# Where the second products stand in the slots of a Gelu expert layer

## The chip, the cores and the metric

The kernel runs on one core of one Trainium2 chip. The metric is the device time of one execution in microseconds (us), taken as the median of several runs. The engines are named as in the profile: PE is the matrix engine (PEld its weight loads), ACT the scalar engine, DVE the vector engine, POOL the engine that adds the accumulators here, SP the queue that issues most of the DMAs.

## The reference

The whole is a two-layer block on an input of 32 images x 256 channels x 14 x 14 in float32: a convolution by codebooks with batch norm, a top-2 mixture of 32 experts, a gated squeeze-and-excite stage, and, last, the expert layer that the change touches. Cut to that layer:

```python
h = x @ Wm + bm                                  # 6272 tokens x 256
t = h.reshape(bs * L_ * H, HD)                   # 8 heads of 32 each
w = softmax(t @ expert_emb)                      # 16 experts
topw, topi = top_k(w, 2)
hmid = gelu(einsum('td,edi->tei', t, W1) + b1)   # 128 hidden numbers for each expert
eo = einsum('tei,eio->teo', hmid, W2) + b2
comb = (take_along_axis(eo, topi) * topw).sum(1)
out = comb.reshape(bs, L_, d) @ Wo + bo
```

## The kernel before

All earlier stages run first. The stage of the change ("Gelu stage") computes all 16 experts for every token and head, and weights the outputs with gates that are zero outside the top two.

**Tiling.** The work is cut into 49 units of 1024 columns (256 tokens x 4 heads; the last one 128 tokens x 8 heads). A unit has 4 groups of 4 experts, so there are 196 groups (`NG`) and 784 first products (`m` counts them). Each of these is one expert on 1024 columns:

- `first(m)` (L2258): two matmuls of 512 columns into one of three PSUM tiles `psA[m % 3]`. Because there are three tiles, it waits until the Gelu of product m-3 is done (the wait on `Q["gel"]` in L2263).
- The Gelu (ACT, L2326) of 1024 columns, from `psA[m % 3]` into `hid[m % 8]`. Every fourth one first waits until the second products of the group two back are done, because it overwrites their input.
- `second(g, b)` (L2269): the second products of group g for one of two blocks of 512 columns; four experts side by side in four column strips of the array, into `psY[use % 2]`. It needs the four Gelus of its group, and the DVE must have read what stood in that `psY` tile two uses before.
- `weigh` (DVE, L2347): reads `psY`, adds the bias, multiplies with the gates, writes `gacc` or `gsum`. POOL adds these up (L2254).

**Slots.** PE, DVE and SP walk through 201 slots by hand-written order. In slot k PE issues the four first products of group k (here called f0 to f3) and the two second blocks of group k-1 (s0 and s1). Some slots hold more, each through one use of `psY`: a `fold` (L2280, the sum over the four strips, one per unit, after f2), a `last` (L2291, the output product, two per unit pair, after f0), a `route` (L2314, transposing the gates of a later chunk, 14 in this stage, after f0).

**Order in a slot.** `apart(k)` (L2179) says whether a slot's second blocks stand apart. They do in a slot without extras, and in one whose only extra is a fold and whose successor has no `last`: there the order is f0 f1 f2 s0 f3 s1. In all others it is f0 f1 f2 s0 s1 f3. Of slots 3 to 194, whose lengths the prediction adds up, 84 have no extra (all apart), 48 a fold (24 apart), 46 a `last` (none apart), 14 a `route` (none apart).

The loop that issues them on PE:

```python
for e in range(4):
    if k < NG:
        first(4 * k + e)
    ...
    if e == 2 and "fold" in EXTRAS[k]:
        fold(FOLD[k], EXTRA_USE["fold", k])
    for b in range(NB if 0 < k <= NG else 0):
        if e == (2 + b if apart(k) else 2):
            second(k - 1, b)
```

Of the kernel before, what the change touches and what calls it, by code (L numbers as in the profile page):

```python
# [44 lines left out]
def wait(eng, sem, value):  # L45

    if not (isinstance(value, int) and value <= 0):
        eng.wait_ge(sem, value)
# [33 lines left out]
def build(nc, x, c1T, c2T, c3T, invts, lut1, lut2, lut3, bn1, bn2, bn3, routerT, w_moe,  # L82
          se_w1T, se_b1, se_w2T, se_b2, se_wgT, se_bg, wm, bm, emb, w1, b1, w2, b2, wo, bo, out):
    with ExitStack() as ctx:
# [812 lines left out]
        with phase() as c2:  # L897
# [20 lines left out]
            with nc.Block() as block:  # L918
                @block.gpsimd
                def _(eng):  # L920
                    eng.memset(nm[:], 0.0).then_inc(S["one"], 1)
                    eng.wait_ge(S["one"], 1)
                    eng.memset(nm[:].rearrange("p s (q x) -> p (s q) x", x=32)[:, :, 16:18], 1.0).then_inc(S["one"], 1)
                    for t in range(T):
                        wait(eng, S["y"], t + 1)

                        wait(eng, S["nsc"], (t - 1) * 2)
                        eng.tensor_copy(y_r[:, t % 2], y[:, t % 3]).then_inc(S["yr"], 1)
# [727 lines left out]
        def route_pe(eng, r, use):  # L1656

            wait(eng, Q["rt"], (r + 1) * RT2)
            wait(eng, Q["got"], use if r < EARLY else use - 1)
            for s in range(NSUB):  # L1660
                m = eng.transpose(gates_ps(use)[:, s * SUB:(s + 1) * SUB],  # L1661
                                  route_tile(r, M1)[:, s * NH:(s + 1) * NH].rearrange("p h e -> p (h e)"), ident[0:SUB, 0:SUB])
            m.then_inc(Q["put"], 1)
# [486 lines left out]
        LAST = {8 * c + 11 + m_: (c, m_) for c in range(len(PARTS) - 1) for m_ in range(2)}  # L2150
# [18 lines left out]
        EXTRAS, EXTRA_USE, BLOCK_USE, uses = {}, {}, {}, EARLY  # L2169
# [6 lines left out]
                BLOCK_USE[k - 1, b] = uses  # L2176
                uses += 1

        def apart(k):  # L2179

            return not EXTRAS[k] or (EXTRAS[k] == ["fold"] and k + 1 not in LAST)

        def done_group(g):

            return BLOCK_USE[g, NB - 1] + 1 if g >= 0 else 0
# [32 lines left out]
        with nc.Block() as block:  # L2218
# [37 lines left out]
            @block.tensor  # L2256
            def _(eng):
                def first(m):  # L2258
                    w = m // 16
                    if m % 16 == 0:  # L2260
                        wait(eng, q_stk[w % 2], (w // 2 + 1) * 64)

                    wait(eng, Q["gel"], m - 2)  # L2263
                    for b in range(NB):
                        mm = eng.matmul(psA[m % 3][:, b * BLK:(b + 1) * BLK], w1_r[:, m % 16],  # L2265
                                        x_r[:, w % 2, b * BLK:(b + 1) * BLK], start=True, stop=True)
                    mm.then_inc(Q["mm1"], 1)

                def second(g, b):  # L2269
                    use = BLOCK_USE[g, b]  # L2270
                    wait(eng, Q["gel"], 4 * g + 4)

                    wait(eng, Q["got"], use - 1)
                    for e in range(4):
                        mm = eng.matmul(psY[use % 2][32 * e:32 * e + 32, :], w2_s[:, g % 4 * 4 + e],  # L2275
                                        hid[:, (4 * g + e) % 8, b * BLK:(b + 1) * BLK], start=True, stop=True,
                                        tile_position=(0, 32 * e))
                    mm.then_inc(Q["put"], 1)

                def fold(w, use):  # L2280
                    tok, n, head, heads = UNITS[w]

                    wait(eng, Q["acc"], 3 * w + 3)
                    wait(eng, Q["got"], use - 1)
                    for q in range(heads):
                        mm = eng.matmul(psY[use % 2][q % 4 * 32:q % 4 * 32 + 32, q // 4 * n:(q // 4 + 1) * n], foldm[:],  # L2286
                                        gacc[:, w % 2, q * n:(q + 1) * n], start=True, stop=True,
                                        tile_position=(0, q % 4 * 32))
                    mm.then_inc(Q["put"], 1)

                def last(c, m_, use):  # L2291
                    n = PARTS[c][1]

                    wait(eng, Q["got"], max(use - 1, EXTRA_USE["fold", 4 * min(2 * c + 1, NU - 1) + 6] + 1))
                    for h in range(2):
                        mm = eng.matmul(psY[use % 2][:, 0:n], wo_s[:, h, m_ * 128:(m_ + 1) * 128], comb[:, h, 0:n],  # L2296
                                        start=(h == 0), stop=(h == 1))
                    mm.then_inc(Q["put"], 1)

                for k in range(SLOTS):  # L2300
                    if k == 1:
                        eng.wait_ge(Q["w2"], 16)
                    if k == min(LAST):
                        eng.wait_ge(Q["wo"], 16)
# [3 lines that stand above are left out]
                        if e == 0 and "last" in EXTRAS[k]:  # L2308
                            last(*LAST[k], EXTRA_USE["last", k])
                        if e == 0 and "route" in EXTRAS[k]:  # L2310
                            route_pe(eng, ROUTE[k], EXTRA_USE["route", k])
                        if e == 2 and "fold" in EXTRAS[k]:
                            fold(FOLD[k], EXTRA_USE["fold", k])
                        for b in range(NB if 0 < k <= NG else 0):  # L2314
                            if e == (2 + b if apart(k) else 2):
                                second(k - 1, b)

            @block.scalar
# [109 lines left out]
```

## Time and profile before

| | |
|---|---|
| median of 3 runs | 2380.0 us (2377.41 to 2391.9) |
| span of the profiled execution | 2466.2 us |
| PE busy | 2088.2 us, 85% of the span |
| DVE busy | 1331.5 us, 54% |
| ACT busy | 1290.4 us, 52% |
| POOL busy | 818.1 us, 33% |
| Gelu stage, first to last Gelu | 1560.8 to 2455.9 us |

The profiled execution has no time of its own beside its span; it is 86 us (3.6%) longer than the median of the runs. The Gelu stage is a good third of the span. In it PE and ACT are both nearly always busy, so a share of busy time does not tell which of them sets the pace; the order of single instructions does.

### The profile page before, as it was taken

To read this page: it belongs to the slowest core of one execution; us is meant where nothing else is said; L and a number is where in the kernel's file an instruction comes from. 1 tells how busy PE (TensorE), PEld (TensorE's weight loads), DVE (VectorE), ACT (ScalarE), POOL (GpSimd) and SP (SyncE) were. 2 spreads that over 40 slices of the span, in tenths; PEclk is the share of its full clock that TensorE was granted. 3 is DMA by queue.
4 is the path that set the end of the run, shared out by engine and by line. 5 is a ranking of instruction groups with operands and counts; after the bars stand their busy time and mean duration, and the time that the engine had idled before them with its cause. 6 is when DMAs were issued, how large, how long until landed. Compare 5 with 4: busy or idle time off the path is not lost. (4 is left out here: it accounts for less than half of the span.)

```text
span 2466.2 us, 36023 instructions
## 1 busy us (share of the span) xinstructions
PE 2088.2 (85%) x12850; PEld 1155.0 (47%) x12851; DVE 1331.5 (54%) x2117; ACT 1290.4 (52%) x1634; POOL 818.1 (33%) x608
## 2 busy tenths in 40 slices
PE   6998699997975653788289887799999999999998
PEld 3444355554544442577155554344444444444443
DVE  5666435554555554122166675366666766666633
ACT  2444222222542221122134342698989989988997
POOL 4332211120005554000657511234434334334343
PEclk8999779998996665899578896899999999999999
DMA  2010211212523331576323311555565655556554
GB/s 54 27 34 8 85 59 59 69 55 85 198 89 107 104 100 43 161 209 198 95 64 114 105 59 60 143 162 158 163 162 153 163 155 159 159 160 163 155 151 117
DMA packets 280563, 281.24 MB, mean 114 GB/s; under 512 B 44998, under 2 KB 261654, under 8 KB 280278
## 3 DMA queue, kind: packets, MB, share of 16 engines
q1 hardware_dynamic: 246422, 233.49, 33.8%
q0 software_dynamic: 12288, 25.72, 3.5%
q10 hardware_dynamic: 21696, 19.93, 2.4%
q8 instruction: 99, 1.62, 0.3%
q14 instruction: 58, 0.48, 0.1%
HBM read 203.76 MB, written 75.25 MB: 113 GB/s over the span
## 5 line engine op out<-in xcount | busy, mean ns | idle before, releaser
L2326 ACT ACTIVATE BIG<-psA,b_s 128x1024 f32<-128x1024 f32 x784 | 809.8, 1116 | 89.8 <-PE psA L2265 82.2
L2254 POOL TENSOR_TENSOR BIG<-BIG 128x1024 f32<-128x1024 f32 x147 | 359.6, 2446 | 553.1 <-DVE BIG L2347 553.1
L2265 PE MATMUL psA<-x_r,w_r 128*128 128x512 f32 x1568 | 480.4, 427 | 20.4 <-DMA x_r<-hs_d 12.2
L2347 DVE SCALAR_TENSOR_TENSOR BIG<-psY,b_s,BIG 128x512 f32<-128x512 f32 x392 | 291.6, 749 | 247.6 <-PE psY L2275 246.8
L2265 PEld LDWEIGHTS psA<-x_r,w_r 128*128 128x128 f32 x1568 | 269.0, 190 | 330.5 <-ACT BIG L2326 244.9
L2275 PE MATMUL psY<-BIG,w_s 128*32 128x512 f32 x3136 | 400.9, 602 | 2.9 <-DVE BIG L2347 2.2
L1199 POOL DMA_INDIRECT xg_d<-xnb,SLOT x128 | 131.6, 1028 | 144.2 <-issue 75.4
L719 DVE TENSOR_REDUCE b_nm<-psN 112x32 f32<-112x512 f32 x128 | 83.1, 686 | 148.3 <-PE psN L616 147.8
L1774 POOL DMA_INDIRECT gath<-yg_d,SLOT x128 | 129.9, 1015 | 83.8 <-issue 42.9
L2275 PEld LDWEIGHTS psY<-BIG,w_s 128*32 128x32 f32 x3136 | 73.6, 108 | 160.9 <-issue 91.3
L719 DVE TENSOR_REDUCE a_nm<-psN 98x32 f32<-98x512 f32 x128 | 82.3, 685 | 90.8 <-PE psN L607 90.6
L1535 PE MATMUL ps<-BIG,xv 128*128 x528 | 127.1, 384 | 2.6 <-ACT xv L1561 2.0
L557 POOL CAST b_pat_r<-BIG 72x3584 fp32r<-72x3584 f32 x16 | 50.8, 3172 | 219.7 <-PE psN L616 212.4
L1561 ACT ACTIVATE xv<-ps 128x512 f32<-128x512 f32 x66 | 39.4, 597 | 156.9 <-PE ps L1521 156.9
L580 PE MATMUL ps<-BIG,b_wb 72*128 72x392 f32 x256 | 100.9, 540 | 3.9 <-DVE xv L725 3.9
L1535 PEld LDWEIGHTS ps<-BIG,xv 128*128 128x128 f32 x528 | 96.2, 192 | 14.5 <-issue 3.9
L775 ACT ACTIVATE b_exs<-ps 128x1568 f32<-128x1568 f32 x32 | 47.3, 1477 | 104.5 <-PE ps L585 104.5
L616 PE MATMUL psN<-b_wb_r,b_pat_r 73*112 73x128 f32 x512 | 70.7, 285 | 9.6 <-POOL b_pat_r L557 8.9
L1454 PE MATMUL psN<-ones_c,MS 98*32 98x1 f32 x128 | 6.7, 182 | 82.2 <-DVE MS L1269 72.2
L1576 DVE COPY ex<-ps 128x512 f32<-128x512 f32 x33 | 22.8, 692 | 99.0 <-PE ps L1535 99.0
L616 PEld LDWEIGHTS psN<-b_wb_r,b_pat_r 73*112 73x112 f32 x512 | 61.1, 193 | 30.6 <-DVE b_nm L719 13.4
L1521 PE MATMUL ps<-ident,xv 128*128 128x128 f32 x264 | 41.5, 282 | 39.8 <-DMA xv<-xg_d 25.0
(394 smaller groups left out, 3242.9 us busy)
## 6 DMA issues: line engine op xcount, KB each, us to landing
BIG<-wt_d SPq DMA_DIRECT2D x784, 128.0 KB, 3.2
x_r<-hs_d SPq DMA_DIRECT2D x196, 128.0 KB, 3.5
xg_d<-ex SPq DMA_DIRECT2D x64, 264.0 KB, 3.6
xv<-xg_d SPq DMA_DIRECT2D x66, 256.0 KB, 3.1
BIG<-ypad_d SPq DMA_DIRECT2D x140, 120.0 KB
xv<-x SPq DMA_DIRECT2D x64, 196.0 KB, 2.6
hs_d<-xv SPq DMA_DIRECT2D x32, 392.0 KB
yg_d<-ex ACTq DMA_DIRECT2D x33, 256.0 KB, 3.6
```

The lines of the kernel that those rows point to most:

```text
L557: eng.tensor_copy(pat_r[0:KP].rearrange("p g (b r) -> p g b r", b=IMGS), pat[s % 3][:, :, :, 0:HH * PADW]).then_inc(S["vr"], 1)
L580: eng.matmul(ps4[:, i, 0:CH], w_, src, start=True, stop=False)
L616: mm = eng.matmul(psN[0:SR, bank, g * 128:(g + 1) * 128], pat_r[0:KR, bank * 4 + g, sub * SR:(sub + 1) * SR], wb_r[0:KR, bank * 4 + g], st ...
L719: eng.tensor_reduce(dst, src, AX.X, ALU.max, negate=True).then_inc(S["max"], 1)
L1199: eng.indirect_dma_start(xg_d.ap(), bass.IndirectOffsetOnAxis(ap=SLOT[:, t * NSUB + s, j:j + 1], axis=0), xnb[:, t % XB, s], None).then_in ...
L1535: m = eng.matmul(psZ[:, u, r * C:(r + 1) * C], xt[:, u, r, h * 128:(h + 1) * 128], w_moe_s[:, bass.ds(e * (2 * C) + h * C, C)], start=(h = ...
L1774: eng.indirect_dma_start(gath[:, c % GB, 2 * s + j], None, yg_d.ap(), bass.IndirectOffsetOnAxis(ap=SLOT[:, c * NSUB + s, j:j + 1], axis=0) ...
L2254: eng.tensor_tensor(gacc[:, w % 2], gacc[:, w % 2], gsum[:, a % 2], ALU.add).then_inc(Q["acc"], 1)
L2265: mm = eng.matmul(psA[m % 3][:, b * BLK:(b + 1) * BLK], w1_r[:, m % 16], x_r[:, w % 2, b * BLK:(b + 1) * BLK], start=True, stop=True)
L2275: mm = eng.matmul(psY[use % 2][32 * e:32 * e + 32, :], w2_s[:, g % 4 * 4 + e], hid[:, (4 * g + e) % 8, b * BLK:(b + 1) * BLK], start=True, ...
L2326: eng.activation(hid[:, m % 8], psA[m % 3][:], ACT.Gelu, bias=b1_s[:, m % 16:m % 16 + 1]).then_inc(Q["gel"], 1)
L2347: eng.scalar_tensor_tensor(out=dst, in0=psY[use % 2][:], scalar=b2_s[:, g % 4:g % 4 + 1], in1=wb[:, g % 3, b * BLK:(b + 1) * BLK], op0=ALU ...
```

## The change

The function `apart` goes, and with it the distinction between slots. In every slot both second blocks are issued behind the fourth first product: f0 f1 f2 f3 s0 s1. The extras stay where they were (a `last` or a `route` behind f0, a `fold` behind f2, so now ahead of f3). No instruction is added or removed, and no wait is changed; the uses of `psY`, the order on DVE, POOL, ACT and SP stay as they are.

```diff
-        def apart(k):
-
-            return not EXTRAS[k] or (EXTRAS[k] == ["fold"] and k + 1 not in LAST)
-
...
                         if e == 2 and "fold" in EXTRAS[k]:
                             fold(FOLD[k], EXTRA_USE["fold", k])
                         for b in range(NB if 0 < k <= NG else 0):
-                            if e == (2 + b if apart(k) else 2):
+                            if e == 3:
                                 second(k - 1, b)
```

## Rows read from the trace of the kernel before

**Rows 1.** The page: busy shares, and the chain that ended last by line.

```profile
PE 2088.2 (85%) x12850; PEld 1155.0 (47%) x12851; DVE 1331.5 (54%) x2117; ACT 1290.4 (52%) x1634; POOL 818.1 (33%) x608
PE psA L2265 16%; PE psY L2275 15%; PE psY L2296 2%; ACT BIG L2326 1%; PE psY L2286 1%; DMA rt<-ex_d 0%; PE psY L1661 0%; SPq L2215 0%; SPq L2205 0%; POOLq L2218 0%; POOL BIG L2254 0%; DVE BIG L2347 0%; DVE rs L1625 0%; DVE ex L2356 0%; SPq L2225 0%
```

**Rows 2.** Busy time by stretch: us, then each engine, TensorE's granted clock, DMA.

```profile
54.00:250.00 196.00, 177.61 (x1721) 95.38 (x1720) 125.96 (x159) 85.72 (x117) 59.31 (x50) 0.99 0.08 22
925.00:1014.00 89.00, 32.87 (x166) 26.97 (x166) 28.34 (x85) 10.54 (x21) 31.01 (x32) 0.55 0.22 66
1017.00:1180.00 163.00, 137.69 (x728) 113.38 (x726) 43.07 (x63) 35.84 (x60) 4.83 (x12) 0.98 0.69 202
1577.00:2451.00 874.00, 865.43 (x5239) 382.56 (x5237) 540.88 (x713) 793.11 (x768) 353.27 (x145) 1.00 0.59 157
```

**Rows 3.** Timeline of PE from 2099.81 us on: start, length, instruction and count.

```profile
2099.81 1.67 PE L2265 MATMUL psA<-x_r,w_r 128*128 128x512 f32 x6
2101.41 0.64 PE L2286 MATMUL psY<-BIG,fold 128*32 128x256 f32 x8
2101.87 1.04 PE L2275 MATMUL psY<-BIG,w_s 128*32 128x512 f32 x8
...
2104.50 1.67 PE L2265 MATMUL psA<-x_r,w_r 128*128 128x512 f32 x6
...
2107.76 1.06 PE L2275 MATMUL psY<-BIG,w_s 128*32 128x512 f32 x8
2108.75 1.67 PE L2265 MATMUL psA<-x_r,w_r 128*128 128x512 f32 x6
2110.35 1.07 PE L2275 MATMUL psY<-BIG,w_s 128*32 128x512 f32 x8
2111.35 0.73 PE L2265 MATMUL psA<-x_r,w_r 128*128 128x512 f32 x2
2112.01 1.06 PE L2275 MATMUL psY<-BIG,w_s 128*32 128x512 f32 x8
2113.01 0.74 PE L2265 MATMUL psA<-x_r,w_r 128*128 128x512 f32 x2
...
2114.97 1.92 PE L2275 MATMUL psY<-BIG,w_s 128*32 128x512 f32 x16
2116.83 1.66 PE L2265 MATMUL psA<-x_r,w_r 128*128 128x512 f32 x6
2118.76 0.74 PE L2265 MATMUL psA<-x_r,w_r 128*128 128x512 f32 x2 [0.27 <-ACT BIG L2326]
```

**Rows 4.** Timeline of PE, a slot with a last and the slot behind it.

```profile
2126.49 1.20 PE L2265 MATMUL psA<-x_r,w_r 128*128 128x512 f32 x4
2127.53 1.02 PE L2296 MATMUL psY<-ex,wo_s 128*128 128x256 f32 x4
2128.20 1.28 PE L2265 MATMUL psA<-x_r,w_r 128*128 128x512 f32 x4
2129.41 1.92 PE L2275 MATMUL psY<-BIG,w_s 128*32 128x512 f32 x16
2131.27 1.67 PE L2265 MATMUL psA<-x_r,w_r 128*128 128x512 f32 x6
2133.21 0.74 PE L2265 MATMUL psA<-x_r,w_r 128*128 128x512 f32 x2 [0.28 <-ACT BIG L2326]
2133.88 1.06 PE L2275 MATMUL psY<-BIG,w_s 128*32 128x512 f32 x8
```

**Rows 5.** Timeline of ACT, the Gelus of the same slots; in brackets the idle time before.

```profile
2105.33 11.64 ACT L2326 ACTIVATE BIG<-psA,b_s 128x1024 f32<-128x1024 f32 x11 [0.56 <-PE psA L2265]
2117.59 4.13 ACT L2326 ACTIVATE BIG<-psA,b_s 128x1024 f32<-128x1024 f32 x4 [0.62 <-PE psA L2265]
```

**Rows 6.** Timeline of ACT, the first Gelu of slot 3 and of slot 195.

```profile
1577.39 1.12 ACT L2326 ACTIVATE BIG<-psA,b_s 128x1024 f32<-128x1024 f32 x1 [0.73 <-PE psA L2265]
...
2451.06 3.12 ACT L2326 ACTIVATE BIG<-psA,b_s 128x1024 f32<-128x1024 f32 x3
```

**Rows 7.** Timeline of PE, PEld and DVE, slot 34, which has a fold.

```profile
1717.61 0.64 PE L2286 MATMUL psY<-BIG,fold 128*32 128x256 f32 x8
...
1718.06 2.16 PE L2275 MATMUL psY<-BIG,w_s 128*32 128x512 f32 x16
1718.59 0.41 DVE L2356 COPY ex<-psY 128x256 f32<-128x256 f32 x1
1719.12 0.19 PEld L2275 LDWEIGHTS psY<-BIG,w_s 128*32 128x32 f32 x8 [0.93 <-ACT BIG L2326]
```

**Rows 8.** Timeline of DVE: both weighs of a slot, and a routing step.

```profile
2130.65 1.51 DVE L2347 SCALAR_TENSOR_TENSOR BIG<-psY,b_s,BIG 128x512 f32<-128x512 f32 x2 [1.57 <-PE psY L2275]
...
2132.78 2.38 DVE L1636 TENSOR_TENSOR rt<-rt,rs 98x512 f32<-98x512 f32 x1
```

## The prediction

> **What bounds the kernel now.** I first read the page: PE is the busiest engine, and the chain that ended last runs through PE alone in the Gelu stage, half first products (16% of the span), half second products (15%), with 1% of Gelus [rows 1]. That is not enough, since in this stage ACT works 793 us of 874 and PE's records cover 865 [rows 2]. So I went to the timeline and looked at starts, not at durations, because matmuls overlap.
>
> A plain slot (no extra, order f0 f1 f2 s0 f3 s1) can be read there without a gap: three first products at 2108.75, s0 at 2110.35, f3 at 2111.35, s1 at 2112.01, the next f0 at 2113.01 [rows 3]. That is 1.60 + 1.00 + 0.66 + 1.00 = **4.26 us**, and no idle time stands beside a row: PE sets the pace. ACT could go faster: four Gelus in a row take 4.13 us to the last one's end, one takes 1.12 [rows 5, 6], so their starts lie (4.13 - 1.12)/3 = 1.00 apart and four need 4.01.
>
> A first product costs more alone than in a run, (1.67 - 0.73)/2 = 0.47 for each one added to a run against 0.66 from its start to the next second block [rows 3]; both second blocks in a row take 1.86 (2114.97 to 2116.83) against 2 x 1.00 apart [rows 3]. Changing between the two kinds costs PE time, and the old order changes twice as often as the new one.
>
> The granted clock is 1.00 over the whole stage, the higher of its two levels, 2.4 GHz [rows 2].
>
> **The change part by part.** *PE's work.* The new plain slot is three first products up to a change, 1.60, one more in the run, 0.47, both blocks, 1.86: 3.93 us, a third of a microsecond less than now. If PE or ACT alone set the pace, the slot would fall to about 4.01.
>
> *The new chain.* But f3 may not start before the Gelu of f0 is done (three `psA` tiles), and now both blocks queue behind f3 in PE's order, and the next slot's f0 behind them. So a ring closes once per slot: f3, s0, s1, next f0, its Gelu, next f3. In the old order each ring passes through only one block. Its links, from rows of slots that already have both blocks together:
> - f3 alone to the start of s0: 0.67 (2133.21 to 2133.88, a first product that also came out of a wait on ACT) [rows 4];
> - s0 to the next first product: 1.86 [rows 3];
> - f0 to the start of its Gelu: 0.83 (2104.50 on PE, 2105.33 on ACT, ACT idle before) [rows 3, 5];
> - start of a Gelu to the first product that waits for it: 1.17 (2117.59 to 2118.76, PE idle 0.27 before) [rows 3, 5].
>
> Together **4.53 us**, above both 3.93 and 4.01: the ring sets the pace, and PE waits some 0.6 us a slot ahead of f3. A plain slot gets 0.27 longer. The third link is the uncertain one: for the Gelu after 2116.83 it is 0.76 (to 2117.59), but that one isn't the first of its group and has no second wait [rows 3, 5]; I take 0.83, with 0.76 as the lower bound (4.46).
>
> *Slots with a route* (14). Today f0, route, f1, f2 take 1.96 (2113.01 to 2114.97) [rows 3]; with f3 in the run and both blocks PE needs 1.96 + 0.47 + 1.86 = 4.29, less than the ring, so 4.53.
>
> *Slots with a fold* (48). f0 to fold is 1.60 and the fold takes 0.46 until s0 (2101.41 to 2101.87), its records 0.64 [rows 3]. How long from a fold to a first product isn't shown; between these, say 0.55. Then f3 starts 2.15 behind f0, where the ring alone would let it at 0.83 + 1.17 = 2.00. The slot is 4.53 + 0.15 = 4.68 (4.59 to 4.77). The apart ones take 4.69 now (2099.81 to 2104.50) [rows 3], so nothing changes there. The others gain: with both blocks directly behind the fold, s1 waits for the DVE's copy of the fold where that is late, as in slot 34, where the weights of the second block start at 1719.12 after a copy at 1718.59 [rows 7]; behind f3 that copy is done in time.
>
> *Slots with a last* (46). PE is the bound there: 4.78 from 2126.49 to 2131.27 [rows 4]. In the new order f0 to last is 1.04 - 0.47 = 0.57, last to the end of f1 f2 1.88, f3 0.47, the blocks 1.86, also 4.78; f3 starts about 2.35 behind f0, later than the 2.00 of the ring, so the ring has slack and nothing changes.
>
> *What else is moved.* No DMA, no wait and no DVE, POOL or SP instruction changes its place; the uses of `psY` keep their order. s1 still ends the slot, so the Gelu that waits for s1 to free `hid`, and the gates that SP loads, see it at the same place in the slot. I cost these at nothing; DVE's reading of `psY` is a rival below. What PE saves in changes (0.33 a slot) ends in its wait ahead of f3. In the last slots, before the drain, f3 comes ahead of the blocks, which is worth under 1 us once.
>
> *The sum.* From the first Gelu of slot 3 to that of slot 195 the profile has 2451.06 - 1577.39 = 873.67 us [rows 6], 192 slots. Afterwards: 84 + 14 slots at 4.53 = 443.9, 48 at 4.68 = 224.6, 46 at 4.78 = 219.9, together 888.4. The difference is **+14.7 us** on a span of 2466.2, 0.6%. So the plain slots lose some 0.25 on 84, and a third of it comes back in folds and routes that already had the bad order. Bounds: the third link at 0.76 takes 6.9 off, the fold's ends 4.3 either way, so +3.5 to +19.
>
> The span is 3.6% above the median of 2380.0, and I can't see in it where unprofiled runs save. Spread evenly, 14.7 becomes 14, and the forecast is **2394 us**. If it is the hand-overs between engines that the profile stretches, the ring (4.53 x 0.965 = 4.37) shrinks while PE's 4.26 stays: 98 x 0.16 = 16 off, about -1, or 2379.
>
> **The rivals.**
> *PE's saving counts.* If the ring's hand-overs were so short that it closes in 4.01, ACT would be the bound in 98 slots: 98 x 0.52 = 51 us less than in my sum and thus 36 below now, 2344. To be faster by 1% the ring has to close below some 4.14, that is 0.39 less than the rows give. Against it: the slots with both blocks together already show ACT idle 0.62 ahead of a Gelu and PE idle 0.28 ahead of a first product [rows 4, 5]; for it, only that a profile may stretch hand-overs.
>
> *The clock falls.* PE now waits in every plain slot. If that dropped TensorE to 1.2 GHz in stretches, PE's 3.93 would approach 7.86, 3.3 above the ring; with a tenth of the 98 slots hit, 33 us come on top of 14, 2427 us. It decides from some 3 slots (10 us) onwards, the point at which the time passes +1%. For it: in the stretch from 925 us, where PE is busy 32.87 of 89, the clock is 0.55. Against it: from 1017 us PE is busy 137.69 of 163, 84%, at 0.98, and from 54 us 91% at 0.99 [rows 2]; the new slot would be at 3.93/4.53 = 87%. The Trainium skill ("TensorE: Matmul & The Clock Gate", A second HAM failure mode: psum-queue depth-cycling) speaks against the change here: frequent short idles of PE between groups of matmuls, as the PSUM tiles are cycled, can make the clock oscillate. The stretches named bear it out little.
>
> *`psY` holds up the blocks.* With s0 and s1 together, both weighs come together on DVE, 1.24 behind s0 (2129.41 to 2130.65), 1.51 for both [rows 4, 8]. The next s0 comes 4.53 behind this one and needs the first weigh, done at 1.24 + 0.75 = 1.99: 2.54 to spare. A routing step takes up to 2.38 between weighs [rows 8]; two of the longest in a slot (4.76) against DVE's free 4.53 - 1.51 = 3.02 leave it 1.74 late, which the slack covers. Beyond 2.54 each microsecond late is one of the slot; 1 us on a quarter of the slots would be some 45 us, 2439.
>
> That the order isn't what the diff says can be set aside: e is 3 once per slot, also in the last ones without first products.
>
> **How the numbers follow.** The ring as costed, +0 to +22 us with the bounds above and some scatter: 0.76. A ring slower by another 0.1 or more, from links that these rows don't show in a steady sequence: 0.09, about 2406. The clock: 0.04. `psY`: 0.05. PE's saving counts: 0.06, of which most ends beyond 1% faster. Runs before spread over 2377 to 2392, so about 1% (24 us) is what a measurement of this kernel can tell from no change, and my 0.6% lies within it. The range is 2374 to 2410: below by the shrunken ring and some scatter, above by the slower ring. Faster by over 1%: 0.05; slower by over 1%: 0.18; within: 0.77.
>
> **What would show it.** In the profile of the changed kernel: plain slots 4.5 from f0 to f0, one run of four first products split by a wait on ACT of some 0.6 ahead of f3, and then sixteen records of second products together; ACT idle some 0.5 ahead of the first Gelu of a slot, nowhere else; slots with a `last` unchanged at 4.78; those with a fold near 4.68 throughout, without the long one of slot 34; PE busy less, the granted clock still 1.00. Plain slots near 4.0 without a wait ahead of f3 would prove me wrong on the ring; waits of second products on DVE, or clock under 1.00, would show the other two rivals.

## The result and the profile after

The changed kernel takes **2398.08 us** (median of 17 runs, 2385.23 to 2410.16), the kernel before 2381.77 (17 runs, 2372.6 to 2392.79). The ratio is 1.0059, with a 95% interval of 1.0043 to 1.0074: slower by 14 us, 0.6% (the medians themselves lie 16 apart). 2394 had been forecast.

The span of the changed kernel's profile is 2408.3 us, 58 *less* than that of the profile before, although the kernel is slower. A comparison of whole spans would mislead here: the first Gelu comes at 1560.8 us in the one and at 1489.2 in the other, and all code ahead of it is the same. Most of that lies in one place of the page, POOL's idle time ahead of the indirect DMAs of an earlier stage. The first row is of before, the second of after:

```profile
L1199 POOL DMA_INDIRECT xg_d<-xnb,SLOT x128 | 131.6, 1028 | 144.2 <-issue 75.4
```

```profile
L1199 POOL DMA_INDIRECT xg_d<-xnb,SLOT x128 | 135.2, 1057 | 80.7 <-issue 74.9
```

All other profiles of this study have 80.5 to 81.0 there, so it is the shown execution of the kernel before that was unusual. What can be compared is the stretch from the first Gelu of slot 3 to that of slot 195, as in [rows 6]. After, in ACT's timeline (start, length, instruction, idle time before):

```profile
1503.50 1.11 ACT L2322 ACTIVATE BIG<-psA,b_s 128x1024 f32<-128x1024 f32 x1 [1.68 <-PE psA L2261]
...
2391.78 1.12 ACT L2322 ACTIVATE BIG<-psA,b_s 128x1024 f32<-128x1024 f32 x1 [0.55 <-PE psA L2261]
```

2391.78 - 1503.50 = 888.28 us, against 873.67 before: **+14.6**, as much as the whole measured difference.

Where it lies is seen in PE's timeline, to be read beside [rows 3, 4] (two plain slots, one with a route, one with a fold, one with a `last`):

```profile
2041.33 0.73 PE L2261 MATMUL psA<-x_r,w_r 128*128 128x512 f32 x2 [0.33 <-ACT BIG L2322]
2042.00 1.92 PE L2271 MATMUL psY<-BIG,w_s 128*32 128x512 f32 x16
2043.85 1.67 PE L2261 MATMUL psA<-x_r,w_r 128*128 128x512 f32 x6
2045.86 0.73 PE L2261 MATMUL psA<-x_r,w_r 128*128 128x512 f32 x2 [0.33 <-ACT BIG L2322]
2046.52 1.92 PE L2271 MATMUL psY<-BIG,w_s 128*32 128x512 f32 x16
2048.37 0.73 PE L2261 MATMUL psA<-x_r,w_r 128*128 128x512 f32 x2
2048.94 0.50 PE L1661 MATMUL psY<-ident,rt 98*128 98x98 f32 x4
2049.22 1.89 PE L2261 MATMUL psA<-x_r,w_r 128*128 128x512 f32 x6
2051.04 1.92 PE L2271 MATMUL psY<-BIG,w_s 128*32 128x512 f32 x16
2052.89 1.67 PE L2261 MATMUL psA<-x_r,w_r 128*128 128x512 f32 x6
2054.49 0.64 PE L2282 MATMUL psY<-BIG,fold 128*32 128x256 f32 x8
2055.06 0.73 PE L2261 MATMUL psA<-x_r,w_r 128*128 128x512 f32 x2
2055.72 1.92 PE L2271 MATMUL psY<-BIG,w_s 128*32 128x512 f32 x16
2057.58 0.73 PE L2261 MATMUL psA<-x_r,w_r 128*128 128x512 f32 x2
2058.15 1.02 PE L2292 MATMUL psY<-ex,wo_s 128*128 128x256 f32 x4
2058.82 1.75 PE L2261 MATMUL psA<-x_r,w_r 128*128 128x512 f32 x6
2060.51 1.92 PE L2271 MATMUL psY<-BIG,w_s 128*32 128x512 f32 x16
2062.36 0.73 PE L2261 MATMUL psA<-x_r,w_r 128*128 128x512 f32 x2
```

The reader sees f0 f1 f2 at 2043.85, then f3 alone at 2045.86, released by a Gelu, then both blocks, and the next f0 at 2048.37: 4.52 us. f3 could have started at 2043.85 + 3 x 0.47 = 2045.26; PE waited 0.60 for it (the row shows 0.33, since it counts from the modelled end of f2). The slot with a fold takes 2057.58 - 2052.89 = 4.69, and no wait stands ahead of its f3; the slot with a `last` 2062.36 - 2057.58 = 4.78, without a wait too.

The same slots on ACT:

```profile
2044.68 4.13 ACT L2322 ACTIVATE BIG<-psA,b_s 128x1024 f32<-128x1024 f32 x4 [0.39 <-PE psA L2261]
2049.20 4.13 ACT L2322 ACTIVATE BIG<-psA,b_s 128x1024 f32<-128x1024 f32 x4 [0.38 <-PE psA L2261]
...
2058.41 1.12 ACT L2322 ACTIVATE BIG<-psA,b_s 128x1024 f32<-128x1024 f32 x1 [0.55 <-PE psA L2261]
2059.68 3.12 ACT L2322 ACTIVATE BIG<-psA,b_s 128x1024 f32<-128x1024 f32 x3 [0.15 <-PE psA L2261]
```

Four Gelus in a row, then idle time ahead of the first of the next slot. All links of the ring can be read off: f3 2045.86, s0 2046.52 (0.66), f0 2048.37 (1.85), its Gelu 2049.20 (0.83); and from a Gelu at 2044.68 to f3 at 2045.86, 1.18.

The stage by stretch, to set beside the last of [rows 2] (us, then busy time of PE, PEld, DVE, ACT, POOL, granted clock, DMA):

```profile
1503.00:2392.00 889.00, 860.56 (x5237) 390.41 (x5236) 545.36 (x714) 798.52 (x769) 352.69 (x145) 1.00 0.58 155
```

PE's records cover 860.56 of 889, a little less than before, and the clock stays at its upper level. In the list of waits of this stretch PE waits on ACT alone, never on DVE:

```profile
PE psA L2261 <- ACT BIG L2322: 28.4, 84, 0.6
```

(in total, times, longest): 84 times, ahead of f3 in each of the 84 plain slots. In the slots with a route the wait is too short for the list.

### The profile page after: what moved, and what is told of

It reads as the page before. It is cut to its first block and busy times, and to the rows that moved or that the text cites. A ratio compares the mean times of both kernels' runs of the same rounds, so it can differ in the third digit from the quotient of the medians.

```text
span 2408.3 us, 36023 instructions
## 1 busy us (share of the span) xinstructions
PE 2090.2 (87%) x12850; PEld 1168.3 (49%) x12851; DVE 1340.0 (56%) x2117; ACT 1295.5 (54%) x1634; POOL 829.3 (34%) x608
## 5 line engine op out<-in xcount | busy, mean ns | idle before, releaser
L2271 PE MATMUL psY<-BIG,w_s 128*32 128x512 f32 x3136 | 377.1, 598 | 1.2 <-ACT BIG L2322 1.2
L2271 PEld LDWEIGHTS psY<-BIG,w_s 128*32 128x32 f32 x3136 | 81.9, 109 | 190.2 <-issue 130.4
L1774 POOL DMA_INDIRECT gath<-yg_d,SLOT x128 | 138.9, 1085 | 57.0 <-issue 42.2
L1576 DVE COPY ex<-ps 128x512 f32<-128x512 f32 x33 | 22.8, 692 | 100.4 <-PE ps L1535 96.9
L580 PEld LDWEIGHTS ps<-BIG,b_wb 72*128 72x128 f32 x256 | 50.3, 207 | 41.5 <-DVE xv L725 8.6
```

The source lines that it names most:

```text
L580: eng.matmul(ps4[:, i, 0:CH], w_, src, start=True, stop=False)
L1774: eng.indirect_dma_start(gath[:, c % GB, 2 * s + j], None, yg_d.ap(), bass.IndirectOffsetOnAxis(ap=SLOT[:, c * NSUB + s, j:j + 1], axis=0) ...
```

## Experiments

The theory: PE's own work sets the pace of the plain slots before (4.26), a ring f3, s0, s1, next f0, its Gelu, next f3 sets it after (4.52), and extras that lie between f0 and f3 hide the wait. Its rivals: PE's work alone decides in both kernels; ACT's total work decides; the place of the blocks in the slot counts as such. All edits but the last are to the changed kernel. "Sum" is the time from the first Gelu of slot 3 to that of slot 195 in the profile, lengths of slots are distances between the first Gelus of neighbours, and times are medians beside the kernel before on the same chip.

**1. Both blocks apart everywhere.**

```diff
-                            if e == 3:
+                            if e == 2 + b:
```

> Both blocks apart in every slot (f0 f1 f2 s0 f3 s1), those with extras too. If the ring over both blocks is what lengthened the plain slots, they go back to PE's own 4.26 us, and slots with a last, where PE is the bound, pay the two added changes: 0.57 + 1.88 + 1.00 + 0.66 + 1.00 = 5.11 instead of 4.78. Routes 4.62, folds 4.69. Over slots 3 to 194: 84 x 4.26 + 14 x 4.62 + 48 x 4.69 + 46 x 5.11 = 882.7 us, 9 above the kernel before (873.7) and 6 below the changed one. If PE's changes between the two kinds cost nothing in the slots with a last, these stay at 4.78 and the sum is 867.

Measured: 2390.97 us against 2382.0, ratio 1.0034 (1.0012 to 1.0057), sum 882.1. Plain slots 4.25, routes 4.62, folds 4.69, slots with a `last` 5.11 to 5.12. Such a slot in PE's timeline, from f0 to the next f0:

```profile
2043.69 0.73 PE L2261 MATMUL psA<-x_r,w_r 128*128 128x512 f32 x2
2044.26 1.02 PE L2292 MATMUL psY<-ex,wo_s 128*128 128x256 f32 x4
2044.94 1.28 PE L2261 MATMUL psA<-x_r,w_r 128*128 128x512 f32 x4
2046.15 1.06 PE L2271 MATMUL psY<-BIG,w_s 128*32 128x512 f32 x8
2047.14 0.74 PE L2261 MATMUL psA<-x_r,w_r 128*128 128x512 f32 x2
2047.81 1.06 PE L2271 MATMUL psY<-BIG,w_s 128*32 128x512 f32 x8
2048.81 1.67 PE L2261 MATMUL psA<-x_r,w_r 128*128 128x512 f32 x6
```

No wait in it: the 0.33 over 4.78 is PE changing between the two kinds twice more. So changes cost PE time where PE is the bound: this order is good for plain slots and bad for those with a `last`.

**2. Both blocks behind f2 everywhere.**

```diff
-                            if e == 3:
+                            if e == 2:
```

> Both blocks behind f2 in every slot (f0 f1 f2 s0 s1 f3): the same work for PE as in the changed kernel, another ring: f2, s0, s1, f3, the Gelu of f3, next f2. That Gelu has no second wait, so the third link is 0.76 and not 0.83: plain and route slots 4.46. The fold now lies inside the ring: 4.46 + 0.46 = 4.92 or more where s1 waits for the copy of the fold. Slots with a last 4.78. Sum 98 x 4.46 + 48 x 4.92 + 46 x 4.78 = 893 us, 5 above the changed kernel and 20 above the one before. If it were not a ring but only the place of both blocks at the end of the slot, plain slots would go to 4.0 to 4.26.

Measured: 2401.72 us, ratio 1.0082 (1.0049 to 1.0114), sum 891.8. Plain and route slots 4.44 to 4.47, folds 4.89 to 4.90, `last` 4.78. PE does the same work in the same runs as in the changed kernel; what differs is which Gelu the ring passes through and what lies inside it. So it isn't the place at the end of the slot as such that costs: the blocks no longer stand there, and plain slots stay far above the 4.0 to 4.26 expected for that case.

**3 and 4. Half a Gelu, inside the ring and outside it.** Both leave out half the columns of one Gelu in four; ACT loses the same work in both. This is the edit of the first; the second has `m % 4 == 2` in its place.

```diff
-                    eng.activation(hid[:, m % 8], psA[m % 3][:], ACT.Gelu,
+                    n = BLK if m % 4 == 0 else NB * BLK
+                    eng.activation(hid[:, m % 8, 0:n], psA[m % 3][:, 0:n], ACT.Gelu,
```

> The changed kernel with the Gelu of the first product of each slot (m % 4 == 0) on 512 of its 1024 columns; the other half is left out, so the output is incomplete. This Gelu is a link of the ring. By the mean durations 1.116 (1024 columns) and 0.584 (392 columns, L1950) a Gelu of 512 takes some 0.69, so the ring closes in 4.10 instead of 4.52: 84 plain slots lose 0.42, 14 routes 0.23, folds and lasts nothing: some 38 us less than the changed kernel, 2360. If the ring isn't the bound but PE or the hand-over of psY, nothing changes.

> The same halving for the third product of each slot (m % 4 == 2), the other half left out too. ACT's work falls by just as much as with the first product, but this Gelu isn't in the ring: plain slots stay at 4.52 and the time at that of the changed kernel, 2398. If ACT's total work set the pace, it would fall as much as with the first product, some 38 us.

Measured: with the Gelu of f0 halved 2353.25 us against 2380.27 (2 runs, ratio 0.9885, 0.9836 to 0.9934), sum 849.2, 39.1 below the changed kernel; with that of f2 halved 2398.73 against the same 2380.27 (ratio 1.0084, 1.0058 to 1.0109), sum 888.3, the same as the changed kernel. ACT in the first, then in the second:

```profile
2041.04 3.71 ACT L2323 ACTIVATE BIG<-psA,b_s 128x512 f32<-128x512 f32 x4 [0.39 <-PE psA L2261]
2045.14 3.70 ACT L2323 ACTIVATE BIG<-psA,b_s 128x512 f32<-128x512 f32 x4 [0.39 <-PE psA L2261]
```

```profile
2030.94 3.70 ACT L2323 ACTIVATE BIG<-psA,b_s 128x1024 f32<-128x1024 f32 x4 [0.82 <-PE psA L2261]
2035.45 3.70 ACT L2323 ACTIVATE BIG<-psA,b_s 128x1024 f32<-128x1024 f32 x4 [0.81 <-PE psA L2261]
```

In both the four Gelus take 3.70. In the first the slot follows (4.10), in the second it stays (4.51) and the gap grows from 0.39 to 0.81. ACT's total work isn't the bound, and neither is PE's, which is the same in both; the one Gelu that lies in the ring counts. The slots with a route add a check of PE's own work: in the first run the ring falls below it, and they take 4.28, where the prediction summed 4.29 for PE.

**5. Each slot in the order that suits its bound.** Apart without extras, both behind f3 with extras.

```diff
-                            if e == 3:
+                            if e == (3 if EXTRAS[k] else 2 + b):
```

> Each slot in the order that its own bound asks for: apart in slots without extras (PE bound at 4.26), both behind f3 in slots with an extra, where the extra already lies between f0 and f3 and hides the wait. Expected 84 x 4.26 + 14 x 4.53 + 48 x 4.68 + 46 x 4.78 = 865.7 us, 8 below the kernel before (a ratio of 0.997) and 23 below the changed one. If the order of one slot carries over into the next, plain slots behind a last stay at the 4.31 of the kernel before and the gain is some 6.

Measured: **2374.14 us** (12 runs) against 2382.0, ratio 0.9972 (0.995 to 0.9994), sum 865.5. Plain slots 4.25, also behind a `last`; routes 4.52, folds 4.68 to 4.69, `last` 4.78. It is faster than the kernel before by 8 us (0.3%), and its sum is 22.8 below that of the changed kernel.

**6. ACT's two waits in the other order.**

```diff
+                    wait(eng, Q["mm1"], m + 1)
                     if m % 4 == 0:
                         wait(eng, Q["put"], done_group(m // 4 - 2))
-                    wait(eng, Q["mm1"], m + 1)
```

> The changed kernel with ACT's two waits ahead of the first Gelu of a slot in the other order: first for its product, then for the second blocks that free its target. If the extra wait is why this hand-over takes 0.83 where others take 0.76, and the order matters, plain and route slots fall to 4.46 and the time by some 7 us. If both waits cost in any order, nothing changes.

Measured: 2391.96 us against 2380.27, ratio 1.0039 (1.0014 to 1.0064), sum 881.9, 6.4 below the changed kernel. Plain slots 4.46. The hand-over from f0 to its Gelu, on PE and on ACT:

```profile
2040.92 1.67 PE L2261 MATMUL psA<-x_r,w_r 128*128 128x512 f32 x6
```

```profile
2041.69 4.13 ACT L2322 ACTIVATE BIG<-psA,b_s 128x1024 f32<-128x1024 f32 x4 [0.34 <-PE psA L2261]
```

0.77 instead of 0.83, so 0.06 of the third link hangs on the order alone. The trace shows what the order does. Of the two waits, the one that is written second becomes an instruction of its own ahead of the Gelu. In the changed kernel that is the wait for the product, which is met last: it stands at 2049.14, and the Gelu starts 0.06 behind it, at 2049.20. Here it is the wait for the second blocks, met early: it stands at 2041.05, and the Gelu, 0.64 behind it, waits for its product itself.

**7 and 8. More work for PE, after and before.** The third first product is issued twice in plain slots, in the changed kernel and in the kernel before.

```diff
-                    for b in range(NB):
+                    for b in [*range(NB)] * (2 if m % 4 == 2 and m >= 16 and not EXTRAS[m // 4] else 1):
```

> The changed kernel with the third first product issued twice in the plain slots from slot 4 on (the same numbers into the same tile, so the output stays). PE gets 0.47 more work in 83 slots, ahead of the wait of f3. By the ring that wait of some 0.6 takes it up: plain slots stay at 4.52 or within 0.05 of it, and the time rises by less than 4 us. If PE's own work set the pace, it would rise by 83 x 0.47 = 39 us, to 2437.

> The kernel before with the third first product issued twice in the plain slots from slot 4 on, as it was done to the changed kernel (where plain slots stayed at 4.52 and the stage at 887.7 us). Here PE has no wait to take it up: by PE as the bound the plain slots go from 4.25 to 4.72 and the time rises by 83 x 0.47 = 39 us, a little less where the slots behind a last had some slack, to about 2418. If ACT or a hand-over set the pace of the kernel before, it stays within a few us of 2381.

Measured: in the changed kernel 2397.83 us (sum 887.7, against 888.28, so nothing), in the kernel before 2426.43 against 2380.86 (2 runs, ratio 1.0202, 1.0141 to 1.0263; sum 910.7, 37.1 more). The medians of the latter lie 46 apart, on two runs; the sum is the firmer number. PE in the changed kernel, one plain slot and the start of the next:

```profile
2064.49 2.73 PE L2261 MATMUL psA<-x_r,w_r 128*128 128x512 f32 x10
2067.15 1.92 PE L2271 MATMUL psY<-BIG,w_s 128*32 128x512 f32 x16
2069.01 2.74 PE L2261 MATMUL psA<-x_r,w_r 128*128 128x512 f32 x10
```

and in the kernel before, one plain slot:

```profile
2050.53 2.14 PE L2265 MATMUL psA<-x_r,w_r 128*128 128x512 f32 x8
2052.59 1.06 PE L2275 MATMUL psY<-BIG,w_s 128*32 128x512 f32 x8
2053.59 0.73 PE L2265 MATMUL psA<-x_r,w_r 128*128 128x512 f32 x2
2054.25 1.06 PE L2275 MATMUL psY<-BIG,w_s 128*32 128x512 f32 x8
2055.24 2.14 PE L2265 MATMUL psA<-x_r,w_r 128*128 128x512 f32 x8
```

After, ten matmuls fit where eight did, and the slot stays at 2069.01 - 2064.49 = 4.52. Before, the slot grows to 2055.24 - 2050.53 = 4.71, by the 0.46 of the added product. In the kernel before PE's work is the bound, in the changed one it is not.

## Why the prediction was right

Slot by slot, measured as in the experiments:

| kind of slot (of 192) | before | forecast | after |
|---|---|---|---|
| plain (84) | 4.25, behind a `last` 4.31 | 4.53 | 4.52 |
| route (14) | 4.45 to 4.77 | 4.53 | 4.52 |
| fold (48) | 4.69 to 4.75; 24 ahead of a `last` 4.84 to 5.11 | 4.68 | 4.68 to 4.69 |
| `last` (46) | 4.77 to 4.78 | 4.78 | 4.78 |
| sum | 873.67 | 888.4 | 888.28 |

The sum and the mechanism came as forecast, kind by kind, and the time within 4 us; what the account had wrong lies in side terms, named below.

- *PE bounds the plain slots before, by changes between the kinds too*: shown by run 8 and, for the changes, by run 1.
- *The ring takes over*: shown by runs 3 and 4 and by the links read in the trace after, 0.66 + 1.85 + 0.83 + 1.18. What PE saves in changes ends in its wait ahead of f3, as forecast; run 7 fills that wait at no cost. That in the old order "each ring passes through only one block" holds for the slots with the blocks apart; in the others the ring f2, s0, s1, f3, its Gelu, next f2 already passed through both, as in run 2.
- *The third link at 0.83 rather than 0.76*: right, and the order of ACT's two waits is its cause (run 6). With it at 0.77 the sum is 881.9; the prediction's lower end for this link gives 888.4 - 6.9 = 881.5.
- *A fold to f3 at 0.55*: 0.57 (2054.49 to 2055.06). The late copy ahead of s1 [rows 7] is gone, as forecast: folds are 4.68 to 4.69 throughout. But it is only part of why folds ahead of a `last` took longer before. It was late in six of the 24 (5.09 to 5.11); in the others, 4.84 to 4.90, the sixteen records of both blocks take 1.90 and not the 2.16 of slot 34, as here:

```profile
2119.88 1.90 PE L2275 MATMUL psY<-BIG,w_s 128*32 128x512 f32 x16
```

  In 11 of the others (4.84) the place at which slots are measured makes the difference. From f0 to f0 on PE these folds take 4.46 before and 4.69 after, while the plain slot that follows the two `last` in nine of the 11 takes 4.69 to 4.70 before and 4.52 after. What came back there came back in that plain slot, where f2 waited 0.28 for a Gelu [rows 4], and not in the fold. The sum is right all the same, since it adds up the new slots alone.
- *Slots with a `last` unchanged*: right. Small miss: I expected ACT idle only ahead of the first Gelu of a slot; in these slots 0.15 also stands ahead of the second.
- *The lower end, in which the profile stretches hand-overs*: did not come. The surplus of the profile of before lay mostly ahead of the indirect DMAs, and the stage costs as much in unprofiled runs (+16 between the medians) as in profiled ones (+14.6).
- *The clock and `psY`*: neither came; granted clock 1.00 through the stage with a wait of PE in every plain slot, no wait of PE on DVE. What the Trainium skill reports of another kernel ("TensorE: Matmul & The Clock Gate", A second HAM failure mode: psum-queue depth-cycling), that short idles between groups of matmuls can make the clock oscillate, isn't borne out here: 0.60 of idle in the 4.52 us of a plain slot left the clock where it was. For `psY` the prediction misread one row: a routing step takes up to 2.75 in the profile of before, not 2.38:

```profile
1713.28 2.75 DVE L1644 TENSOR_TENSOR rt<-rt 98x512 f32<-98x512 f32 x1
```

  Two such steps in a slot (5.50) against DVE's free 3.02 would have left it 2.48 late, nearly all of the 2.54 of slack.
- *What a measurement can tell*: the prediction held that about 1% is the least. With 17 runs of each kernel the interval of 1.0043 to 1.0074 tells 0.6% from no change.

Some slots of the stage's start differ between profiles and were kept out of the sums. Two plain slots of the changed kernel (47 and 175) take 4.80, 0.6 us more in all. In both, the first Gelu of the next slot starts 0.34 behind ACT's separate wait instruction (see run 6), where it is 0.06 elsewhere. The kernel before has the same delay at the same two slots (4.53 each), but there the next slot makes up for it (4.00 to 4.01); in run 6, where the separate wait is met early, it doesn't show. What holds the Gelu up there is not shown.

## What to carry to other kernels

Putting work of one kind together saved PE its changes, a third of a microsecond a slot, but a wait that now stands ahead of the larger block is passed on to everything queued behind it: add up the ring through the other engine and back, once per turn, and compare it with each engine's own work. The longest of these is the pace, so the same edit can pay in slots that have other work between producer and consumer and cost in those that don't; choose the order by slot. Compare profiles by the stretch that the change touches, not by their spans.

## What the runs showed of the hardware

- On ACT the order of two waits ahead of an instruction counts. The one written second ran as an instruction of its own; when that was the one met last, the hand-over from PE took 0.83 us, otherwise 0.77.
- Changing between runs of full-width and of strip matmuls and back costs PE 0.33 us (a slot with a `last` 5.11 against 4.78, measured in run 1; for a plain slot 4.25 measured against the estimate of 3.93, added up from the rows).
- A Gelu on half the columns shortened the ring by 0.42 us (4.52 to 4.10), as much as four Gelus in a row got shorter (4.13 to 3.70 or 3.71).
